# Group norm, channel norm, projection and gate on one core: statistics moved between two engines, and a longer chain of small operations

## The reference

```python
g = gn(x)                              # 32 groups of 4 channels, mean and variance over all pixels
u = mean(g, axis=1); v = var(g, axis=1, ddof=1)      # per pixel, over the 128 channels
n = (g - u) / (sqrt(v) + 1e-6)
n = einsum('bchw,oc->bohw', n, W) + b                # a 128 x 128 projection of the channels
out = g + g * n
```

## Time and profile before

| what | value |
|---|---|
| median of 3 runs | 1874.69 us (1874.65 to 1875.2) |
| the profiled execution | 1875.25 us, its span 1873.4 us |
| granted tensor clock | 0.997 of full |
| PE busy | 1695.9 us (91%) |
| DVE busy | 1695.0 us (90%) |
| ACT busy | 1481.7 us (79%) |
| POOL busy | 1455.2 us (78%) |
| moved by DMA | 667.33 MB, mean 356 GB/s |
| loads of tiles | 752 of 512 KB (64 for each of 8 batches, and 30 streamed again) |
| stores | 512 of 512 KB |

### The profile page before, as it was taken

The page is one execution under the profiler, slowest core; times in us unless marked ns, Lnnn a source line. Parts: engine busy times, 40 slices in busy tenths (PEclk is TensorE's granted clock), DMA queues, the critical chain, the costliest instruction groups (busy, mean ns, idle before and its releaser), DMA issues.

```text
span 1873.4 us, 67650 instructions
## 1 busy us (share of the span) xinstructions
PE 1695.9 (91%) x28706; PEld 918.7 (49%) x28706; DVE 1695.0 (90%) x2000; ACT 1481.7 (79%) x2634; POOL 1455.2 (78%) x1684
## 2 busy tenths in 40 slices
PE   0069999999999999999999999999999999999998
PEld 0045555555555555555555555555555555555553
DVE  5659998999989998999989999999999999888887
ACT  5689887888878887898878889788887988744442
POOL 0058888887888888788788788887887888888885
PEclk9999999999999999999999999999999999999999
DMA  9979999999999999999999999999999999854775
GB/s 375 409 271 370 379 382 329 400 390 397 367 326 413 387 390 349 361 416 378 390 329 395 402 384 379 336 402 389 391 357 356 416 379 398 301 209 188 272 269 216
DMA packets 183037, 667.33 MB, mean 356 GB/s; under 512 B 20560, under 2 KB 20944, under 8 KB 182736
## 3 DMA queue, kind: packets, MB, share of 16 engines
q1 hardware_dynamic: 109008, 394.54, 56.8%
q10 hardware_dynamic: 73728, 268.47, 35.9%
HBM read 394.49 MB, written 268.44 MB: 354 GB/s over the span
## 4 chain that ended last, share of the span: by engine, by line
PE 66%; DVE 15%; issue 6%; DMA 6%; POOL 3%; ACT 2%; SPq 2%; POOLq 0%; ACTq 0%; DVEq 0%
PE proj_ps L749 39%; PE sums_ps L737 15%; PE factor_ps L723 12%; DVE scaled L648 5%; DVE bn L693 4%; DVE bn L694 4%; DMA tiles<-x 4%; SPq L413 2%; DMA out<-tiles 2%; DVE tiles L662 1%; POOL tiles L458 1%; POOL tiles L447 1%; ACT unused L515 1%; ACT squares L575 0%; POOL pieces L477 0%
## 5 line engine op out<-in xcount | busy, mean ns | idle before, releaser
L749 PE MATMUL proj_ps<-scaled,w_t 128*32 128x512 f32 x8192 | 984.9, 598 | 0.1
L458 POOL TENSOR_SCALAR tiles<-tiles,columns_sb 128x1024 f32<-128x1024 f32 x512 | 575.0, 1123 | 231.4 <-DVE tiles L662 227.9
L662 DVE SCALAR_TENSOR_TENSOR tiles<-proj_ps,columns_sb,tiles 128x1024 f32<-128x1024 f32 x512 | 643.6, 1257 | 73.2 <-PE proj_ps L749 71.8
L515 ACT ACTIVATE unused<-tiles,bn 128x1024 uint8<-128x1024 f32 x560 | 635.1, 1134 | 0.0
L648 DVE TENSOR_TENSOR scaled<-tiles,factor_ps 128x1024 f32<-128x1024 f32 x512 | 619.1, 1209 | 10.7 <-PE factor_ps L723 6.5
L447 POOL TENSOR_SCALAR tiles<-tiles,columns_sb 128x1024 f32<-128x1024 f32 x512 | 617.1, 1206 | 13.8 <-DMA tiles<-x 12.8
L575 ACT ACTIVATE squares<-tiles 128x1024 f32<-128x1024 f32 x512 | 537.7, 1050 | 66.1 <-PE sums_ps L737 30.7
L737 PEld LDWEIGHTS sums_ps<-tiles,const_sb 128*32 128x32 f32 x8192 | 245.2, 111 | 317.1 <-issue 263.0
L749 PEld LDWEIGHTS proj_ps<-scaled,w_t 128*32 128x32 f32 x8192 | 213.5, 109 | 360.7 <-issue 306.6
L723 PE MATMUL factor_ps<-pieces,pick_sb 128*128 128x128 bf16 x4096 | 317.7, 220 | 63.3 <-DVE scaled L648 48.4
L737 PE MATMUL sums_ps<-tiles,const_sb 128*32 128x128 f32 x8192 | 319.8, 274 | 13.4 <-ACT squares L575 13.4
(11 more groups left out here) (58 smaller groups left out, 769.6 us busy)
## 6 DMA issues: line engine op xcount, KB each, us to landing
tiles<-x SPq DMA_DIRECT2D x752, 512.0 KB, 8.5
out<-tiles ACTq DMA_DIRECT2D x512, 512.0 KB, 7.1
const_sb<-const SPq DMA_DIRECT2D x1, 86.0 KB, 1.9
scaled<-w SPq DMA_DIRECT2D x1, 64.0 KB, 2.1
scaled<-ident SPq DMA_DIRECT2D x1, 64.0 KB, 2.0
pick_sb<-pick SPq DMA_DIRECT2D x1, 8.0 KB, 1.8
columns_sb<-bias SPq DMA_DIRECT2D x1, 0.5 KB, 2.4
```

The costliest lines, as they stand in the source:

```text
L458: nc.gpsimd.tensor_scalar(place(s), place(s), 1.0, out_shift[:, 0:1], ALU.mult, ALU.add).then_inc(finished, 1)
L515: nc.scalar.activation(unused[:, which, :], data, (ACT.Identity, ACT.Square)[which], bias=pivot_of(of), scale=-1.0, accum_out=act_sums[:, ...
L662: nc.vector.scalar_tensor_tensor(out=place(s), in0=proj_ps[:, s % 2, :], scalar=gate_shift[:, 0:1], in1=place(s), op0=ALU.add, op1=ALU.mul ...
L749: mm = nc.tensor.matmul(proj_ps[q:q + 32, s % 2, h:h + BANK], w_t[:, q:q + 32], scaled[:, s % 2, h:h + BANK], start=True, stop=True)
```

## The change

Statistics: `STATS_DVE` goes from 24 to 18, so 46 tiles fall to ACT. ACT takes them in pairs: one activation reads two tiles (128 x 2048) and adds them into one sum, Identity in one pass and Square in another, so 46 passes a batch. A pass waits until both tiles are loaded and until the pass before it is done, since all write the same `unused` tile. Chain: four steps (`CHAIN_STEPS`). Root, eps and square of the root stay in phase 1 on ACT; the reciprocal and GpSimd's three operations move to phase 2 (`LAG_INVERSE`); factor and pieces to phase 3; the first spread is in phase 0 of the next set. Everything behind (scale, project, gate, store) lies one step later. ACT's statistics pass between its two roundings is gone, and so is the one ahead of the squared sums. The factor is written over `var`, so DVE waits for the `pieces` of the set before ahead of L672. Buffers: 33 tiles kept, 31 streamed; plan constants `STATS_LEAD` 1, `LOAD_GAP` 0.6, and another order in which buffers are tried.

```diff
-KEPT = 34
+KEPT = 33
-STATS_DVE = 24
+STATS_DVE = 18
-CHAIN_STEPS = 3
+CHAIN_STEPS = 4
-LAG_ROOT, LAG_FIT = LAG_VAR + 1, LAG_VAR + 2
+LAG_ROOT, LAG_INVERSE, LAG_FIT = LAG_VAR + 1, LAG_VAR + 2, LAG_VAR + 3
-STATS_LEAD = 2
+STATS_LEAD = 1
-LOAD_GAP = 0.64
+LOAD_GAP = 0.6
...
-    passes = 2 * (slots - dve)
+    passes = slots - dve
     at = [PIVOT_STEP + 1 + p * (until - PIVOT_STEP - 1) // passes for p in range(passes)]
-    begun += [(at[p] + 0.5, "act", at[p:p + 2]) for p in range(0, passes, 2)]
+    begun += [(at[p] + 0.5, "act", at[p:p + 2]) for p in range(0, passes, 2) for _ in range(2)]
...
+ORDER = [(p + 36) % BUFFERS for p in range(BUFFERS)]
...
-        factor = sum_sq
+        factor = var
...
-        SUM_SQ_AFTER = 1
+        SUM_SQ_AFTER = 0
...
-                    root_of = set_behind(step, LAG_ROOT, b, own, before)
+                    root_of = set_behind(step, LAG_INVERSE, b, own, before)
...
-                for i, which in todo[:count]:
-                    data = wait_stats_data(act, n, i)
-                    a = of.index[i]
+                for a, which in todo[:count]:
+                    for i in of.pairs[a]:
+                        wait_stats_data(act, n, i)
+                    low, high = sorted(places.buffer["stats", i] for i in of.pairs[a])
...
-                    if n > 0 or done >= 2:
-                        act.wait_ge(act_done, act_before(n) + (done - 1))
+                    if n > 0 or done >= 1:
+                        act.wait_ge(act_done, act_before(n) + done)
-                    nc.scalar.activation(unused[:, which, :], data, (ACT.Identity, ACT.Square)[which], bias=pivot_of(of),
+                    nc.scalar.activation(unused[:, :, :], tiles[:, low:high + 1:high - low, :],
+                                         (ACT.Identity, ACT.Square)[which], bias=pivot_of(of),
                                          scale=-1.0, accum_out=act_sums[:, which, a:a + 1]).then_inc(act_done, 1)
...
                         nc.scalar.activation(piece[:, :], factor[:, :], ACT.Identity, scale=at["rows_bc"]).then_inc(piece_a_done, 1)
-                        statistics(b + 1, step, of, 1)
                         act.wait_ge(rest_done, done)
...
+                        if ready > 1:
+                            dve.wait_ge(pieces_done, ready - 1)
                         nc.vector.tensor_scalar(var[:, :], var_ps(step - LAG_VAR), TINY, 1.0 / (P - 1), ALU.max, ALU.mult)\
...
-                    if (ready := set_behind(step, LAG_ROOT, b, own, before)) is not None:
+                    if (ready := set_behind(step, LAG_INVERSE, b, own, before)) is not None:
                         dve.wait_ge(root_eps_done, ready)
                         nc.vector.reciprocal(approx[:, :], approx[:, :]).then_inc(approx_done, 1)
```

More of the change, by code:

```diff
@@ L121, in __init__ @@
         for k in range(len(kept)):
-            self.put(("stats", drops + k), k)
+            self.put(("stats", drops + k), ORDER[k])
         for s in streamed:
@@ L155, in free @@
     def free(self, kind, i):
-        found = [p for p in range(BUFFERS) if min(self.room(p, (kind, i))) >= 0]
+        found = [p for p in ORDER if min(self.room(p, (kind, i))) >= 0]
         assert found, (kind, i, self.span[kind, i])
@@ L182, in __init__, with at, passes_at @@
         self.bn_slots, self.act_slots = self.engine.count("dve"), self.engine.count("act")
-    def at(self, step, engine):
-        return [(i, p) for i, steps in enumerate(self.steps) if self.engine[i] == engine
-                for p, t in enumerate(steps) if t == step]
+        act = [i for i, engine in enumerate(self.engine) if engine == "act"]
+        self.pairs = [tuple(act[a:a + 2]) for a in range(0, self.act_slots, 2)]
+    def at(self, step):
+        return [i for i, steps in enumerate(self.steps) if self.engine[i] == "dve" and step in steps]
+    def passes_at(self, step):
+        return [(a, which) for a, (i, _) in enumerate(self.pairs)
+                for which, t in enumerate(self.steps[i]) if t == step]
 def norm_gate_kernel(nc, x, w, bias, const, pick, ident, out):
@@ L211, in act_before @@
             return 0
-        return n * (2 * plan.act_slots) + 2 * (first_plan.act_slots - plan.act_slots)
+        return n * plan.act_slots + (first_plan.act_slots - plan.act_slots)
     with ExitStack() as ctx:
@@ L235, in norm_gate_kernel @@
         bn = sb("bn", [P, 2 * plan.bn_slots, 6])
-        act_sums = sb("act_sums", [P, 2, max(plan.act_slots, first_plan.act_slots)])
+        act_sums = sb("act_sums", [P, 2, max(len(plan.pairs), len(first_plan.pairs))])
         gn = sb("gn", [P, 16])
@@ L569, in period @@
                     if nxt:
-                        todo.extend(of.at(step, "act"))
+                        todo.extend(of.passes_at(step))
                     if own:
@@ L623, in gather @@
                     .then_inc(gn_gathered, 1)
[L624 to L625 removed]
+                dve.wait_ge(act_done, act_before(n) + of.act_slots)
+                nc.vector.reduce_sum(gn[:, 2:4], act_sums[:, :, 0:len(of.pairs)], AXIS_X).then_inc(gn_gathered, 1)
             def invert_root(n):
@@ L689, in period @@
                     if nxt:
-                        for i, _ in of.at(step, "dve"):
+                        for i in of.at(step):
                             data = wait_stats_data(dve, b + 1, i)
```

4 lines of the change are left out of this document (1 added, 3 removed).

## The result

The changed kernel took 1886.28 us (median of 6 runs, 1883.77 to 1887.42), the kernel before 1875.31 in the same measurement (6 runs, 1874.65 to 1880.19). The ratio is 1.0052, with a 95% interval of 1.0042 to 1.0062: slower by half a per cent. The forecast was 1851 with a range of 1837 to 1870. The profiled execution took 1886.48 us, its span is 1884.7, the granted clock 0.995 of full.

What follows compares the result with a forecast made beforehand. PE was taken to set the pace at 3.28 us a spread, losing time waiting for DVE's `scaled` in double steps. 1875.25 - 34.9 - 2.1 + 2.4 + 4.9 + 6.3 = 1851.9, against the median 1851, range 1837 to 1870.

Steps and rivals of the forecast that it cites:

- Statistics off DVE: PE's steps with two statistics tiles on DVE: six a period become single, 42 x 0.83 = 34.9 us less; three stay.
- The factor (0.453) fits, so phase 3 starts its gate on time: On DVE between scale and gate: the 0.453 us factor operation fits where DVE waits 0.66 anyway, so no delay.
- Rival 4: On DVE: factor, late from GpSimd, holds phase 3's gate; 77 single steps pay 0.3 each, 1874, no change; 4%.
- The chain: Four-step chain: moved DVE operations fit or their delay dies before the next gate; one added pipeline step costs 2.4 us.
- The wait for the pieces of the set before: On DVE ahead of L672: pieces are due before phase 0's spread, earlier than L672 runs, so 0 us.
- The price of a pass: ACT's 128 x 2048 statistics pass: 1.98 us, within bounds of 1.134 and 2.27.
- The term of 4.9 for crowded sets: ACT's sets of four passes, three a period, 1.4 us over each: 0.7 a period taken, +4.9 in all.
- Loads: Streamed tiles late at GpSimd's norm, slots 57 to 63: 0.9 us a period, +6.3; bounds 0 to 3.28 a period.
- rival 1: End of each period: loads late for good, a whole step lost, 23 us in place of 6.3, 1868; 13%.
- Rival 3: DMA engines give no more than the present 378 GB/s: period 221.1 us, time 1887; 4%.
- End of a period: Last steps of each period: pieces no longer hold step 63, spread at about 753.9 instead of 754.24; -2.1 us.

Runs made afterwards that it cites:

- Experiments 5 and 6: Changed kernel with the factor operation's second input in PSUM: 5 with another number (output wrong), 1874.0 us; 6 with right numbers, the reciprocal copied there by ScalarE, 1876.94 us.
- experiment 5: Changed kernel, factor operation's second input read from PSUM (the variance sum, so output is not the reference's): 1874.0 us, ratio 0.9984 to the kernel before.
- Experiment 4: Changed kernel with the next image's moments issued one step later, behind the squared sums of step 60: 1880.53 us, ratio 1.0022 to the kernel before.
- experiment 1: Half of each output tile stored (columns 512 to 1023 not written), in both kernels: changed kernel 1863.1 us, kernel before 1871.38.
- experiment 2: Changed kernel with another buffer plan, 32 tiles kept and statistics asked for two buffers ahead: 1876.49 us, ratio 1.0004 to the kernel before.
- the one with three cures: Changed kernel with 32 kept and statistics asked for earlier, moments one step later, reciprocal copied to PSUM: 1868.35 us; with half of each output tile stored, 1851.22.

## Why the prediction was wrong

Three steps of the prediction failed: the loads, priced at 6.3 us, cost some 20; the factor operation, priced at 0.453 and at nothing behind it, cost 12; and what the longer chain puts in front of what on ACT at the end of a period was not priced and cost 7.5. The other terms came within 3 us.

**Statistics off DVE: right for the steps removed, wrong for those left.** Six of nine double steps went, worth the 34.9 us forecast (34 by the 41 of them that PE's timeline has). The step that failed here is "The factor (0.453) fits, so phase 3 starts its gate on time". It took the mean of an instruction as a property of the instruction. 453 ns was a mixture even then: 0.28 alone, more when GpSimd had a tile under way, up to 1.16. Before, the factor operation started 0.68 us or more into GpSimd's in 113 of 128 sets; in the changed kernel's double steps it starts 0.16 to 0.25 into it. In single steps the spare time took most of it. In double steps the gate starts 0.39 later, and each costs 1.28 and not 0.83: 25.6 us for 20 of them, 9 more than at the old price. Step 59 cost another 2.8. Experiments 5 and 6 show it, and bring the excess of a double step down to 0.91. The 0.08 that stay over 0.83 are not the gate's, which starts on time again; they lie between the start of the scale and PE's next spread (1.34, before 1.26), and their cause is open. Rival 4 named a late factor, but as late input in single steps; nothing was lost in those but at step 59 and a little at steps 31 and 35.

The Trainium skill has the rule ("SBUF — State Buffer", "SBUF: two separate sides"): VectorE and GpSimd share a port pair that is locked for a whole instruction by whoever starts first, and a VectorE operation with two SBUF inputs needs it, against a GpSimd operation that reads SBUF. The trace agrees: 280 to 1164 ns with both inputs in SBUF, 278 to 289 with one in PSUM, and GpSimd's 1.24 in place of 1.12 where DVE was first. The prediction should have weighed this rule; of DVE's operations in a step only this one has two inputs in SBUF.

**The chain.** The first spread stands 2.25 us later, against 2.4 forecast. The wait for the pieces of the set before cost nothing that the timeline shows, as said.

**ACT.** The price of a pass was right to half a per cent, and ACT keeps up on average. The term of 4.9 for crowded sets came to 5.3, all of it at steps 31 to 35, though two other sets are as crowded; experiment 5 takes 1.5 of it away, so that part is the factor's. What the sum lacked is step 60, 7.5 us: the prediction looked at ACT's sums per set and not at what stands behind what where the chain got longer. Experiment 4 shows it.

**Loads.** This term failed most: 6.3 us forecast as an addition, 19 added by experiment 1 (23 less the 4 of the kernel before). The timelines have 24.6 at steps 55 to 57, against 3.8 before. That is rival 1's size, a whole step a period, and the upper bound of the prediction. The prediction looked for lateness at the norm only. There it came, with 24.9 us of waits for 12.8; but it came also at the statistics tiles. ACT reads two at once, so a pass waits for the later of them, and the last pair is first read in step 55, behind which squares and squared sums have no slack. Rival 3, the fixed rate, had the period right at 221.1, and by bytes the changed kernel moves what the old one did: 83.4 MB in 221.1 us and 82.8 in 219.7 are 377 GB/s both. But the rate isn't fixed there: the kernel of experiment 2 moves 83.9 MB in a period of 219.3 (383 GB/s), and the one with three cures moves them in 218.1 (385). And without late transfers, with half stores, the changed kernel's period is 217.6, still 1 to 2 us over the forecast. So rival 3's 1887 is near the time by coincidence: the terms of experiments 4 and 5 have nothing to do with transfers. What was right in it is its direction.

**End of a period.** 5.0 us less against 2.1 forecast.

**The sum, with measured sizes,** in us over the seven periods, by the table above: -24.8 (double steps: 50.4 to 25.6) + 5.3 (steps 31 to 35) + 24.6 - 3.8 (late tiles) + 10.3 (steps 59, 60) - 5.0 (end) + 2.4 (elsewhere) + 2.3 (longer pipeline) = +11.3, which is the difference of the two spans. The double steps' waits that were removed made the period denser, and the transfers, with a share of 0.99 already, didn't follow in the last sets. The prediction saw that share and then priced lateness by the one wait that was there.

**What stays open.** Why buffers come free too late in the last sets even with 32 kept (17 us between full and half stores): order of the queue and rate of the stores were not told apart. Why DVE's factor operation falls where it does within GpSimd's was read and not tested. Wide passes against narrow ones were not tried alone, nor the three-step chain operation by operation.

## What to carry to other kernels

Where the DMA share is near 1, price a shorter period by making the transfers lighter first (half the stores is one line): the two times tell how much of a gain the transfers can take back. Read the minimum of an instruction beside its mean: a spread of 280 to 1164 ns on one shape means that something else holds it, and moving it by a step changes its price. When a chain gets a step longer, list for each engine what now stands between its last and its next operation at the places where rare work (moments, group scalars) is put in.

## What the runs showed of the hardware

- The 128 x 128 factor operation of VectorE, with both inputs in SBUF, ended 0.12 to 0.16 us behind the end of GpSimd's operation on a 128 x 1024 tile whenever that was under way (121 of 128; 381.57 against 381.43, for one). It took up to 1.16 us for the 0.28 that it takes alone. In the other seven it started within 0.06 us of GpSimd's and took 0.29, and GpSimd's L468 took 1.24 or 1.25 for 1.12: each can hold the other. With one of the inputs in PSUM it always took 0.28 or 0.29.
- A copy of the second input to PSUM by ScalarE (0.27 us, 128 times) takes this away: 9.3 us less for the changed kernel, 2.0 when the other two cures are in place.
- At a DMA share of 0.98 to 1.00 the rate was 381 GB/s in one kernel and 387 in another with a different order of loads: here the share didn't tell how much was left.
